# Two tiles to a wait: ScalarE's copies and VectorE's additions of a graph kernel are paired

## The reference

```python
seg = dst * 40 + edge_type
S   = segment_sum(x[src], seg).reshape(n, 40, 128)       # sum of source rows by target and type
cnt = segment_sum(ones, seg).reshape(n, 40)
agg = einsum('nrd,rdf->nf', S, relation_weights) + cnt @ rFeatures
h   = agg * deg_isqrt
h   = relu(h + h @ loop_weight)
out = layernorm(x + h)
```

## Time and profile before

| | us |
|---|---|
| median of 3 runs | 1065.96 (1064.67 to 1066.28) |
| profiled execution | 1067.09 |
| its span | 1065.2 |
| TensorE busy | 963.2 |
| TensorE weight loads busy | 856.5 |
| VectorE busy | 735.1 |
| ScalarE busy | 529.9 |
| GpSimd busy | 788.1 |

### The profile page before, as it was taken

How to read it: one execution, slowest core, us unless ns; L and a number is a source line. 1 busy time by engine, 2 the same in 40 slices (tenths; PEclk the granted TensorE clock), 3 DMA queues, 4 the chain that set the end, 5 groups by cost and what they waited for, 6 DMA issues and landing times.

```text
span 1065.2 us, 26678 instructions
## 1 busy us (share of the span) xinstructions
PE 963.2 (90%) x6713; PEld 856.5 (80%) x6713; DVE 735.1 (69%) x2572; ACT 529.9 (50%) x1119; POOL 788.1 (74%) x832
## 2 busy tenths in 40 slices
PE   3589999998999999999999999999999999989997
PEld 1379988888888788888888888888887888878887
DVE  7687777666766766676667666666766676767663
ACT  3566554454545445544444544455454554444552
POOL 7777777777777777777777777777777777777770
PEclk9779999999999999999999999999999999999999
DMA  8933344434433444444344444444433344333430
GB/s 271 303 89 107 113 114 115 115 113 117 117 115 113 116 115 114 113 117 116 112 117 114 117 113 115 116 115 112 114 112 110 111 114 114 110 112 110 114 112 25
DMA packets 68987, 127.27 MB, mean 119 GB/s; under 512 B 17287, under 2 KB 41582, under 8 KB 68830
## 3 DMA queue, kind: packets, MB, share of 16 engines
q0 software_dynamic: 38400, 103.80, 34.5%
q1 hardware_dynamic: 16398, 15.38, 4.6%
q10 hardware_dynamic: 14032, 6.35, 2.1%
HBM read 115.85 MB, written 9.60 MB: 118 GB/s over the span
## 4 chain that ended last, share of the span: by engine, by line
PE 50%; DMA 25%; POOL 15%; issue 7%; DVE 1%; POOLq 0%; SPq 0%; ACT 0%; DVEq 0%; ACTq 0%
PE win_ps L1103 25%; DMA rows<-x_parts,src 24%; PE agg_ps L1115 21%; POOL rows L557 13%; POOL raw L564 2%; PE win_ps L1141 1%; DMA x_in<-x 1%; PE win_ps L1188 1%; PE win_ps L1089 1%; PE win_ps L1140 0%; POOLq L556 0%; DVE hot L856 0%; SPq L461 0%; DVE ring L989 0%; DMA src<-src_main 0%
## 5 line engine op out<-in xcount | busy, mean ns | idle before, releaser
L557 POOL DMA_INDIRECT rows<-x_parts,src x766 | 732.5, 956 | 234.4 <-issue 156.2
L653 ACT COPY ring<-win_ps 128x451 f32 x831 | 465.7, 560 | 383.1 <-PE win_ps L1103 187.9
L1103 PE MATMUL win_ps<-hot,rows 128*128 128x480 f32 x1634 | 566.1, 431 | 60.9 <-DMA rows<-x_parts,src 53.7
L1115 PEld LDWEIGHTS agg_ps<-ring,w 128*128 128x128 f32 x3936 | 554.2, 191 | 41.9
L1115 PE MATMUL agg_ps<-ring,w 128*128 128x128 f32 x3936 | 562.2, 275 | 0.0
L989 DVE TENSOR_TENSOR ring<-ring,win_ps 128x41 f32 x831 | 188.6, 227 | 307.9 <-DMA rows<-x_parts,src 220.0
L856 DVE TENSOR_SCALAR hot<-iota,key_f 128x480 fp32r<-128x480 f16 x831 | 384.0, 462 | 1.0 <-issue 1.0
L1103 PEld LDWEIGHTS win_ps<-hot,rows 128*128 128x128 f32 x1634 | 251.1, 193 | 98.4 <-DMA rows<-x_parts,src 86.5
L1089 PEld LDWEIGHTS win_ps<-hot_node,hot_type 128*128 128x128 bf16 x831 | 77.1, 100 | 42.0 <-issue 15.7
L1089 PE MATMUL win_ps<-hot_node,hot_type 128*128 128x12 bf16 x831 | 86.0, 171 | 19.9 <-DVE ring L989 12.1
L564 POOL DMA_INDIRECT raw<-x,src x51 | 53.7, 1054 | 15.6 <-issue 14.0
(11 more groups left out here) (93 smaller groups left out, 251.6 us busy)
## 6 DMA issues: line engine op xcount, KB each, us to landing
x_out<-x_parts SPq DMA_DIRECT2D x1674, 1.0 KB
rows<-x_parts,src POOLq DMA_INDIRECT x766
x_parts<-x_out SPq DMA_DIRECT2D x6, 512.0 KB, 6.5
x_parts<-ring SPq DMA_DIRECT2D x6, 512.0 KB, 6.5
out<-out_sb ACTq DMA_DIRECT2D x48, 64.0 KB
x_blk<-x ACTq DMA_DIRECT2D x47, 64.0 KB
w<-relation_w SPq DMA_DIRECT2D x8, 320.0 KB
x_in<-x SPq DMA_DIRECT2D x6, 256.0 KB
```

The costliest lines, as they stand in the source:

```text
L557: pool.indirect_dma_start(rows[0:n, k].rearrange("p c d -> p (c d)").bitcast(F32), None, x_parts, bass.IndirectOffsetOnAxis(ap=src[0:n, t: ...
L653: nc.scalar.copy(ring[:, :, bass.ds(start + 1, WIN - 1)], win_ps[bank_of(t)][:, :, 1:WIN]).then_inc(copied, 1)
L1103: ins = nc.tensor.matmul(banks[bank_of(t)][:, 0:R * WIN], of[:, part], hot[:, t % HOTS], start=False, stop=(part == PARTS - 1), skip_group ...
L1115: ins = nc.tensor.matmul(sums_of(c), w[:, r, :], ring[:, r, bass.ds(seg, BLOCK)], start=(r == 0), stop=(r == COLS - 1))
```

## The change

ScalarE waits once for a pair of tiles (k even) and copies both; only the second copy raises `copied`, by two. VectorE waits once for both copies and once for the gather, adds both tiles, and only the second addition raises `added`, by two. Tile 16 of a block stays alone and raises by one. The gather that VectorE waits for at an even tile t is that of tile t + 6 now, and the odd tile waits for none. In front of the addition of the second tile of a pair stands a drain (an instruction that waits until VectorE's earlier work is finished); `added` is waited on nowhere on VectorE in its place. A drain stands in front of the first tile's too.

```diff
+        def pair_end(i, k):
+            return i * TPB + min(k - k % PAIR + PAIR, tiles_of(i))
...
                         act.drain()
-                        act.wait_ge(tile_done, t + 1)
-                        nc.scalar.copy(ring[:, :, bass.ds(start + 1, WIN - 1)],
-                                       win_ps[bank_of(t)][:, :, 1:WIN]).then_inc(copied, 1)
+                        if k % PAIR == 0:
+                            act.wait_ge(tile_done, pair_end(i, k))
+                        ins = nc.scalar.copy(ring[:, :, bass.ds(start + 1, WIN - 1)], win_ps[bank_of(t)][:, :, 1:WIN])
+                        if t + 1 == pair_end(i, k):
+                            ins.then_inc(copied, k % PAIR + 1)
...
-                        dve.wait_ge(copied, t + 1)
+                        if k % PAIR == 0:
+                            dve.wait_ge(copied, pair_end(i, k))
                         if not known_less(t - 1 + AHEAD, USED):
-                            dve.wait_ge(added, t)
+                            dve.drain()
...
-                        last = min(t + max(BEHIND, LEAD - t // LEAD_STEP), USED - 1)
-                        dve.wait_ge(gather_issued, gathers_through(last))
-                        nc.vector.tensor_tensor(a, a, win_ps[bank_of(t)][:, :, 0:1], ALU.add).then_inc(added, 1)
+                        if k % PAIR == 0:
+                            last = min(t + max(BEHIND + 1, LEAD - t // LEAD_STEP), USED - 1)
+                            dve.wait_ge(gather_issued, gathers_through(last))
+                        ins = nc.vector.tensor_tensor(a, a, win_ps[bank_of(t)][:, :, 0:1], ALU.add)
+                        if t + 1 == pair_end(i, k):
+                            ins.then_inc(added, k % PAIR + 1)
```

## The result

The changed kernel takes 1098.85 us (median of 4 runs, 1098.74 to 1100.55) against 1065.43 us: a ratio of 1.032 (95% interval 1.031 to 1.033), so slower by 3.2%. The forecast was 1086 in a range of 1068 to 1108. The direction and the kind of loss came as forecast. The size did not: 20.6 us were forecast and 33.4 measured, and one step of the sum was plainly wrong.

The account below looks back on a forecast made before the run. GpSimd's gathers were taken to bound the kernel. 1067.1 + 17 (longer gathers in held blocks) + 3 (start and tail) gave 1087 us for the profiled execution, so 1086 for the median, range 1068 to 1108.

Parts of the forecast that it names:

- What bounds the kernel: GpSimd sets the pace from 73 us on: start 72.8, 766 gathers at 1.261 us each, tail 27.5 us.
- The price of an overlap: A one-hot matrix starting 0.34 to 0.08 us ahead of a gather lengthens it by the overlap less 0.13.
- The sum for the second tile: VectorE's unheld second half of each pair, priced by what precedes its matrix: gathers lengthened by 0.33 us a block.
- Then the drain ... I take 0.13: On VectorE between a pair's first matrix and second addition: a drain taking 0.13 us, so the addition starts at 0.62.
- quiet second half: Rival: drain costs nearly nothing, second matrices at 2/3, 8/9, 14/15 stay below 0.91; 1067 to 1070 us, chance 0.13.
- 2/3, 8/9 and 14/15: Pairs with hot_node, y_sb or out_sb in between: second matrix at 0.93 to 0.95, cost 0.02 to 0.05 each.
- past it, 0: Pair 12/13, with a clear of 659 ns: second matrix starts at 1.33, past the bad place, cost 0.
- The place k = 10/11: Pair with y_mid and hot_node in between: second matrix starts at 1.12, cost 0.21 us.
- Late pairs: Pairs 12/13, 0/1 and 4/5 don't get copies in time; up to 0.4 us a block, taken as 0.13.
- ScalarE, TensorE: ScalarE's saved wait is worth nothing; TensorE's additions come 1 to 2 us later, which GpSimd doesn't notice.
- Start and tail: First gather later by 1.5 us, VectorE unheld longer 1 us, tail about 0.5 us: together 3 us, bounds 0 and 6.
- The signs that were named: Mean gather 25 ns longer, worst at k = 10/11; second matrix at +0.76; first gather at 74 us; VectorE's gather waiting halved.

Follow-up runs that it names:

- the two on the other chip: Kernel before with merge also waiting for the gather, and only the gather wait paired with merge behind tile 6's addition, on another chip: 1368.78 and 1362.40 us.
- the edit that costs 3.0% elsewhere: Kernel with only the gather wait paired, merge moved from in front of tile 6's wait to behind its addition: 1096.30 us, ratio 1.030.

## Why the prediction was right where it was, and where it wasn't

**What bounds the kernel: right.** GpSimd's gathers, start and tail make up the time in every run but the two on the other chip, and differences in time are differences in the gathers' busy time: +42.5 us for +44.4, +9.3 for +11.4, +10.6 for +13.6, +31.6 for +33.4 (the rest is start and tail).

**The price of an overlap: right.** Overlap less 0.13, in merge at two places (0.50 and 0.40 of overlap, 0.37 and 0.27 measured) and in `one_hot_types` (0.38, 0.25), each within 0.01. The prediction turned a figure of the Trainium skill the wrong way round, though. In "SBUF — State Buffer", section "A bandwidth-pool intuition that's wrong (but worth ruling out)", the loser is blocked until the other's end and some 115 ns more. A gather blocked so from its start would cost the overlap plus 0.12, not less; the measured cost is the overlap less 0.13, so the rows don't bear the figure out, and 0.13 comes from the earlier trace rows alone.

The Trainium skill, "SBUF — State Buffer", section "Who interferes with whom", says that tensor_tensor takes only the read side of the shared port, and infers that descriptor generation, which needs the write side, is not stalled by it. The trace differs from this inference: merge is a tensor_tensor with both inputs in SBUF and lengthens a gather by 0.37 when it lies across its start. It is in line with the same section's rule that a VectorE instruction with two SBUF inputs contends with a GpSimd instruction that reads SBUF, if a gather counts as one: it takes its row numbers from `src`. Where it lies across the later part (from 0.41 on), it costs nothing, while a matrix there costs 0.05. That a gather reads at its start and writes towards its end would fit both; that is an argument, and no run here shows which port is held.

**The sum for the second tile: wrong, and its total near by luck.** The step "Then the drain ... I take 0.13" priced an instruction that isn't there. The trace of after (a pair off the beat, but the distances within it are those of any pair) shows the second addition starting 0.09 ahead of the first matrix's end, as operations did before (520.35 + 0.46 against 520.72):

```profile
520.35 0.46 DVE L862 TENSOR_SCALAR hot<-iota,key_f 128x480 fp32r<-128x480 f16 x1
520.51 1.11 POOL L561 DMA_INDIRECT rows<-x_parts,src  x1 [0.30 <-issue]
520.72 0.21 DVE L997 TENSOR_TENSOR ring<-ring,win_ps 128x41 f32 x1
520.85 0.46 DVE L862 TENSOR_SCALAR hot<-iota,key_f 128x480 fp32r<-128x480 f16 x1
```

With no drain, my own list would have given 0.03 us a block, that is the "quiet second half" of 1067 to 1070 us. It is refuted: only the gather wait paired costs 44 us. Two things failed beneath it.

The first is that the list put every second half too late, by the 0.13 of the drain and by the 0.09 that the addition overlaps the first matrix. The second matrix of a clean pair (4/5, 6/7) comes at +0.60, forecast were 0.76. At 2/3, 8/9 and 14/15 it comes at +0.72 to 0.75, not 0.93 to 0.95, and is harmless. At 12/13 the list had 1.33, "past it, 0"; there it comes at 1.12 with only the gather wait paired and 1.16 in the changed kernel (medians), which is just ahead of the next gather:

```profile
231.22 0.46 DVE L862 TENSOR_SCALAR hot<-iota,key_f 128x480 fp32r<-128x480 f16 x1
...
231.31 1.19 POOL L561 DMA_INDIRECT rows<-x_parts,src  x1 [0.30 <-issue]
```

So the place priced at nothing costs 0.20 to 0.25 a time: 8.3 us with only the gather wait paired, 4.7 in the changed kernel.

The second is that the list priced only the matrices. The second half of a pair is not just a matrix; behind it come `one_hot_types` (k = 4) and merge (k = 6), placed in front of the next pair's addition, which nothing held any more. In the kernel before they started at a matrix's end, some 0.4 behind a gather's start, by the beat. Now they follow the second matrix, at 1.1 or so, which is a gather's start. They hold 18.5 of the 34.9 us after, and 26.7 of the 46.8 us (counted the same way) where only the gather wait is paired. The place k = 10/11, for which I had 0.21, measured 0.19 in its gathers:

```profile
228.26 0.47 DVE L862 TENSOR_SCALAR hot<-iota,key_f 128x480 fp32r<-128x480 f16 x1
...
228.60 1.15 POOL L561 DMA_INDIRECT rows<-x_parts,src  x1 [0.30 <-issue]
228.63 0.29 DVE L914 CUSTOM_DVE_ANT_0 h_sb<-y_mid 128x128 f32<-128x128 f32 x1
```

but not for my reason: the matrix overlaps by only 0.13, which is free, and the variance (L914) behind it ends at 0.32; 0.32 less 0.12 is the 0.20 that the gather has over 0.95. So here the two count as one. That isn't a general rule. In the traces of twelve kernels the matrix of k = 11 and L914 did so some 150 times, and the matrix of k = 3 and `one_hot_types` 9 times of 15, but the matrix of k = 2 and `one_hot_nodes` at most once in 42; what tells them apart is open. k = 2/3, 8/9 and 14/15, priced at 0.12 a block, 5 us, cost some 1.5.

**Late pairs: right in kind.** The copies in pairs alone make the kernel 13.6 us slower, and gathers 10.6 us longer; half of the latter is the pair 0/1 behind the position load, as the prediction had it. Of the other two pairs that it named, 12/13 costs 0.6 us there. 4/5, which was to be late by the additions' count, costs 1.2 us where that is in pairs too and every tile waits for the gather. 2/3, which it didn't name, costs 2.1 us in either run. In the sum I had 0.13 us a block, 5 us.

**ScalarE, TensorE: right.** Additions counted in pairs cost nothing; GpSimd's idle time stayed at 233.6 us while TensorE waited 106.6 us for additions, so TensorE took its longer waits out of what it had to spare.

**Start and tail: right.** 1.7 and 0.5 us, forecast 1.5 and 0.5.

**The signs that were named.** The mean gather was to grow by 25 ns and grew by 41; the first gather was to come at 74 us and came at 74.5; VectorE's waiting for gathers fell from 220.0 to 205.0 us, not by half, since fewer waits were each longer. The place k = 10/11 was to be the worst and was the third. The second matrix of a clean pair was to stand at +0.76 and stood at +0.60.

## What to carry to other kernels

A wait can be worth more for when it starts an engine than for what it protects. If GpSimd issues gathers as the pacemaker, find where in a gather VectorE's operations with two inputs in SBUF begin, and its fast ones with one input (the matrix of 480 columns takes 0.46 us, the clear of 492 takes 0.66 and does no harm). Keep each from lying across a start; a wait on GpSimd's own progress does this for nothing while VectorE has time to spare. Before thinning out waits, follow everything that stands between one remaining wait and the next, not only the instructions whose waits go; and when reading a diff, check the condition that an instruction stands under.

## What the runs showed of the hardware that was not expected

- How far ahead of a gather an operation may begin depends on the operation. Twelve traces, from 140 us on: one-hot matrices that began 0.01 to 0.04 us ahead cost nothing in over 500 cases, at 0.05 and 0.06 either nothing or 0.27, and from 0.09 on their overlap less 0.13. Merge and `one_hot_types` have no such harmless lead. `one_hot_types` that began 0.03 to 0.05 ahead cost 0.35 to 0.37 in 26 cases, and merge that began 0.01 ahead cost 0.52 (only the gather wait in pairs):

```profile
748.47 0.66 DVE L924 TENSOR_TENSOR ring<-ring 128x492 f32<-128x492 f32 x1
748.48 1.47 POOL L557 DMA_INDIRECT rows<-x_parts,src  x1 [0.30 <-issue]
```

- Merge that begins 0.03 or 0.41 behind a gather's start costs nothing. This one 0.67 us operation, moved by 0.2 us in one run and by 0.7 us in another, is worth 13 and 12 us over 43 blocks.
- A matrix that begins 0.42 to 0.44 or 0.93 to 0.95 behind a gather's start costs 0.06 (30 and 11 cases before, 40 of the second with only the gather wait paired); at 0.6 and 0.75 it costs nothing.
- A clear of 655 ns (a copy with one input) that lies across a gather's start by some 0.5 us costs nothing, in 27 gathers of the changed kernel, while merge of the same length and shape does.
- On one chip the same kernel took 1366 instead of 1065 us, at a granted clock of 0.887 to 0.92 instead of 0.98 to 0.99. GpSimd was not the pacemaker there, and the edit that costs 3.0% elsewhere came out at a ratio of 0.997. TensorE was busy 1061.1 of 1363.6 us in a kernel profiled there, against 963.2 of 1065.2, so its own longer work is some 100 us of the 300; where the other 200 come from is open.
